# Scores of an attention kernel: one head in every second step, or two heads in every fourth

## The chip, the cores and the metric

The kernel runs on one core of a Trainium2 chip. The metric is the device time of one execution in microseconds (us). For the kernel before, three runs are shown, with a median of 1465.92 us.

## The reference

The tokens x are 64 sequences of 32 tokens with 512 features. Each sequence is mixed along its tokens by a 32x32 matrix, picked by a condition. Then come attention with 32 heads of 128 features (queries and keys normalised over all 4096 features), a residual, a linear layer with quantised weights and a low-rank update, and a gated low-rank expert layer with a residual:

```python
x = x + attn(einsum('bct,bcd->bdt', x, W[condition]))   # q, k = rms_norm(h @ Wq + bq), rms_norm(h @ Wk + bk)
                                                        # softmax(q k^T / sqrt(128)) v, then @ Wo + bo
x = x + ffn(cond2(x))                                   # quantised weight + lora; 8 experts, softmax gates
```

What matters here is q k^T: for each head and each sequence, a 32x32 block of scores from 32 queries and 32 keys with 128 features.

## The kernel before, in words

The queries and keys of the 32 heads are computed in 64 steps (`for s in range(N_QK)`, two steps a head, h = s // 2); the values follow in 32 further steps; then come softmax, values times probabilities, the output projection and the last layers. Two steps of a head cover the 2048 tokens, since a step treats a 1024-token half by a scheme of seven products: the 2x2 block product of (query and key weights) by (tokens) is made with seven products of half size instead of eight (p1 to p7, each six matmuls of 128x512 on TensorE: hi and lo parts of the operands, L672), and the results are put together from sums of products. A step delivers four blocks of 128x512: q_lo (block_11, L1687), q_hi (block_12, L1713), k_hi (block_22, L1700) and k_lo (ACT, L1224).

Each engine runs a list in a fixed order, written out by hand, and semaphores tie the lists together:

- TensorE, per step: p6(s), p5(s), p1(s+1), p7(s), in even steps `scores(s // 2 - 1)`, p2(s+1), p4(s), p3(s). `scores(h)` (L791) is 64 products of 128x32 by 128x32, each recorded as two instructions, in four column groups of the array, into bank 3 or 7. It uses the blocks of both steps of head h. In the steps of the values a product is twelve matmuls of 128x256 (L683).
- ACT: keep_a2(s) (L1115, behind p6), square and gain of q_hi(s-1), square and gain of q_lo(s) (L1136, L1142), a split of weights (L1052), keep_a3(s) (L1124, behind p7), keep_a1(s+1) (L1106), square of k_hi(s), k_lo(s).
- DVE: block_12(s-1), one threshold level of the quantised weights (L1653 and L1654, `level`), low_qk(6) in odd steps or low_qk(3) in even ones (L1548), block_22(s), in even steps keep_scores (L1672), low_qk(7) in odd steps, block_11(s+1), in steps with s % 6 == 1 a second level, low_qk(4) or low_qk(1). Steps 2 to 6 have small preparing operations in place of levels (`code_scales`, `code_steps`, `normalised`, `code_order`, `first_level`).
- POOL: in each step the additions of the squares (L1454, `add_square`), and sums of the next weights (`add_qk`).
- SP: loads of weights (`load_raw`) and the stores of scores to memory (`spill`).

p4(s) waits for a3_kept(s), p3(s) for c22_done(s) (block_22). block_22 of an even step waits for `scored`, since it writes over a block of keys that the scores read. Blocks of queries and keys live in `qk` (two of each kind), with a third place for q_lo in `sqst`. `keep_scores` copies a bank to `stage`, SP stores it, and `kept` frees the bank. `lora(0)` in step 3 writes banks 3 and 7 too.

```python
blk = {(name, par): qk[:, (2 * i + par) * 512:(2 * i + par + 1) * 512]
       for i, name in enumerate(("q_lo", "q_hi", "k_lo", "k_hi")) for par in range(2)}
blk["q_lo", 2] = sqst[:, 3, :]
...
def levels_qk(s):
    return 0 if s < 6 or s > 59 else 2 if s > 6 and s % 6 == 1 else 1
```

Of the kernel before, what the change touches and what calls it, by code (L numbers as in the profile page):

```python
# [9 lines left out]
ACT = mybir.ActivationFunctionType  # L10
AX = mybir.AxisListType.X

P = 128
# [71 lines left out]
def build(nc, x_nat, x_tr, cond_w, cond_idx, codebook, wqk, wv_in, wo_in, vecs, bo, w2, scale_log,  # L85
# [4 lines left out]
    with ExitStack() as ctx:  # L90
# [33 lines left out]
        wraw = sb("wraw", [P, 2048])  # L124
        accr = sb("accr", [P, 4096])

        with ExitStack() as mem_a:
# [11 lines left out]
        with ExitStack() as mem_b:  # L139
# [30 lines left out]

        blk = {(name, par): qk[:, (2 * i + par) * 512:(2 * i + par + 1) * 512]
               for i, name in enumerate(("q_lo", "q_hi", "k_lo", "k_hi")) for par in range(2)}
        blk["q_lo", 2] = sqst[:, 3, :]
        acc = accr[:, :].rearrange("p (a n) -> p a n", a=2)
# [228 lines left out]
        def _(sp):  # L403
# [49 lines left out]
            for s in range(1, N_QK):  # L453
                if s % 2 == 1 and (s + 3) // 2 < H:
                    load_raw((s + 3) // 2)
                if s == N_QK - 3:
                    load_v_raw(0, 0)
                if s == N_QK - 2:
                    load_v_raw(0, 1)
                if s % 2 == 0:  # L460
                    sp.wait_ge(kept, s // 2)
                    sp.dma_start(spill[s // 2 - 1], stage).then_inc(spilled, 16)

            sp.wait_ge(kept, H)
            sp.dma_start(spill[H - 1], stage).then_inc(spilled, 16)

# [27 lines left out]
            for s in range(N_QK, N_ST):  # L494
# [19 lines left out]
                if s == N_QK:  # L514
                    store_v(s, 11, c11_done)
                store_v(s, 22, c22_done)
                if u == 1:
# [78 lines left out]
        def _(pe):  # L596
# [176 lines left out]
            def scores(h):  # L773

                dst = bank[3 + 4 * (h % 2)]
                if h >= 2:
                    pe.wait_ge(kept, h - 1)
                if h == 1:
                    pe.wait_ge(lora_used, 2)
# [4 lines left out]
                for n in range(NCH):  # L784
                    s, part = 2 * h + n % 2, ("lo", "hi")[n // 2]
                    q, k = blk["q_" + part, s % (3 if part == "lo" else 2)], blk["k_" + part, s % 2]
                    for t in range(TC):
                        for j in range(NB):
                            cols = slice(t * P + j * C, t * P + (j + 1) * C)
                            at = (n * TC + t) * C  # L790
                            ins = pe.matmul(dst[j * C:(j + 1) * C, at:at + C], q[:, cols], k[:, cols],  # L791
                                            start=True, stop=True)
# [20 lines left out]
            for s in range(N_QK):  # L813
# [13 lines left out]
                p7(s)  # L827
                if s % 2 == 0:
                    scores(s // 2 - 1)
                p2(s + 1)  # L830
                if s == 3:
                    pe.wait_ge(kept, 1)
                    lora(0)
# [35 lines left out]
            p5(N_QK)  # L869
            p6(N_QK)  # L870
            scores(H - 1)
            for s in range(N_QK, N_ST):
# [157 lines left out]
        def _(act):  # L1030
# [23 lines left out]
            def split_v(j, q):  # L1054
# [15 lines left out]
                elif j == 6:  # L1070
                    act.wait_ge(scored, H - 1)
                elif j == 7:
                    act.wait_ge(p_done[3], N_QK)
                else:
                    act.wait_ge(scored, H)
# [64 lines left out]
            def gain(name, s, ready):  # L1140
                q = blk[name, s % (3 if name == "q_lo" else 2)]
                act.activation(q, q, ACT.Copy, scale=vec[:, s // 2, 3:4]).then_inc(ready, 1)  # L1142

            def last_q(s):

                act.wait_ge(c12_done, s + 1)
                square(sq_q_hi(s), 0, s % 2 + 2, blk["q_hi", s % 2], None)

# [39 lines left out]
            for s in range(N_QK):  # L1188
# [8 lines left out]
                act.wait_ge(c11_done, s + 1)  # L1197
                square(sq_q_lo(s), 0, s % 2, blk["q_lo", s % 3], None)
                gain("q_lo", s, gq_lo)
# [19 lines left out]
                act.wait_ge(c22_done, s + 1)  # L1219
                square(sq_k_hi(s), 1, s % 2 + 2, blk["k_hi", s % 2], None)  # L1220
                if s % 2 == 0 and s >= 2 and h + 1 < H:
                    split_qk(1, h + 1)
                act.wait_ge(p_done[4], s + 1)
                act.activation(blk["k_lo", s % 2], bank_a(s)[:, :], ACT.Identity, bias=vec[:, h, 1:2], scale=1.0)\  # L1224
                   .then_inc(c21_done, 1)
# [302 lines left out]
        def _(dve):  # L1528
# [145 lines left out]
            def block_11(s):  # L1674
                dve.wait_ge(p_done[2], s + 1)
                dve.wait_ge(a1_kept, s + 1)
                if s < N_QK:
                    dst = blk["q_lo", s % 3]
                    if s == 2:
                        dve.wait_ge(t_lo, t_at(2, 7))  # L1680
# [8 lines left out]
            def block_22(s):  # L1689
                dve.wait_ge(p_done[5], s + 1)  # L1690
                dve.wait_ge(a3_kept, s + 1)
                if s < N_QK:
                    dst = blk["k_hi", s % 2]
                    if s % 2 == 0:
                        dve.wait_ge(scored, s // 2)
                else:
# [5 lines left out]
            def block_12(s):  # L1702
                dve.wait_ge(p_done[3], s + 1)
                dve.wait_ge(a2_kept, s + 1)
                if s < N_QK:
                    dst = blk["q_hi", s % 2]
                else:
# [43 lines left out]
            for s in range(N_QK):  # L1751
# [32 lines left out]
                if s >= 2:  # L1784
                    block_22(s)
                if s % 2 == 0 and s >= 2:
                    keep_scores(s // 2 - 1)
                if s % 2 == 1 and h + 1 < H:
# [29 lines left out]
            low_v(7)  # L1818
            keep_scores(H - 1)
            low_v(4)  # L1820
# [67 lines left out]
            for s in range(N_QK, N_ST):  # L1888
                u = s - N_QK
                block_22(s)  # L1890
                if s + 1 < N_ST:
                    block_11(s + 1)
# [205 lines left out]
```

## Time and profile before

| what | value |
|---|---|
| median of the runs shown | 1465.92 us (1465.64 to 1467.06) |
| span of the profiled execution | 1464.0 us |
| instructions | 37072 |
| TensorE matmul busy | 1459.2 us, 15683 instructions |
| VectorE (DVE) busy | 1089.7 us (74%) |
| ScalarE (ACT) busy | 726.7 us (50%) |
| GpSimd (POOL) busy | 752.5 us (51%) |
| TensorE clock granted | 1.000 |

The profiled execution gives the span from its first to its last instruction; a device time of its own is not given beside it. The median of the runs lies 1.9 us above the span. TensorE counts as busy while a matmul drains, so its idle time says little, and the starts of its instructions say more. In a timeline row stand the start in us from the beginning of the span, the duration in us, engine, line, operation, what is written and read, shapes and the number of instructions merged, and in brackets the idle time of the engine before it and what ended it.

### The profile page before, as it was taken

How to read it: one execution, taken by the hardware profiler on the slowest of the kernel's cores; microseconds unless marked ns; L12 is line 12 of the kernel's file. 1: busy time of each engine (PE TensorE's matmuls, PEld its weight loads, DVE VectorE, ACT ScalarE, POOL GpSimd, SP SyncE). 2: the span in 40 equal slices, each digit the busy share in tenths (PEclk: the TensorE clock that was granted, in tenths of full speed). 3: DMA queues.
4: the chain of work that ended last, by engine and by line, in shares of the span. 5: the costliest groups of instructions: out<-in, count | busy, mean ns of one | idle time of the engine just before them, and what ended most of it. 6: DMA issues, size and time to landing. Idle time of an engine off the chain costs nothing.

```text
span 1464.0 us, 37072 instructions
## 1 busy us (share of the span) xinstructions
PE 1459.2 (100%) x15683; PEld 1262.6 (86%) x15683; DVE 1089.7 (74%) x1505; ACT 726.7 (50%) x1330; POOL 752.5 (51%) x532
## 2 busy tenths in 40 slices
PE   9999999999999999999999999999999999999999
PEld 8788888888888888888999999999888888888887
DVE  8787868788786877874498889988677676667663
ACT  7767677666767667675333333344443222222221
POOL 7667777787777877775444444454453112112100
PEclk9999999999999999999999999999999999999999
DMA  4211111110111101111433433447474244244230
GB/s 151 66 44 45 38 36 38 45 45 31 37 45 45 44 24 44 45 44 59 153 129 131 143 128 133 137 155 228 151 233 131 83 135 131 74 136 140 73 116 30
DMA packets 106998, 135.28 MB, mean 92 GB/s; under 512 B 6224, under 2 KB 89424, under 8 KB 106320
## 3 DMA queue, kind: packets, MB, share of 16 engines
q1 hardware_dynamic: 105968, 132.49, 27.4%
q8 instruction: 123, 2.02, 0.6%
q10 hardware_dynamic: 864, 0.42, 0.1%
q14 instruction: 43, 0.35, 0.1%
HBM read 86.75 MB, written 46.14 MB: 91 GB/s over the span
## 4 chain that ended last, share of the span: by engine, by line
PE 96%; DVE 2%; ACT 1%; issue 1%; DVEq 0%; POOL 0%; ACTq 0%; POOLq 0%
PE bank L672 39%; PE bank L906 24%; PE bank L683 22%; PE bank L865 4%; PE bank L791 3%; PE bank L934 1%; PE bank L952 1%; PE bank L621 0%; DVE qreg L1654 0%; DVE wa L1548 0%; PE bank L600 0%; DVE xs_lo L1611 0%; DVE qreg L1633 0%; PE bank L963 0%; PE bank L920 0%
## 5 line engine op out<-in xcount | busy, mean ns | idle before, releaser
L672 PE MATMUL bank<-xs_hi,wa 128*128 128x512 f32 x1792 | 563.4, 392 | 0.2
L1454 POOL TENSOR_TENSOR accr<-accr,sqst 128x512 f32<-128x512 f32 x248 | 352.8, 1433 | 148.1 <-ACT sqst L1136 108.4
L672 PEld LDWEIGHTS bank<-xs_hi,wa 128*128 128x128 f32 x1792 | 336.3, 188 | 74.3 <-DVE qk L1700 2.4
L672 PE MATMUL bank<-xs_lo,wa 128*128 128x512 f32 x896 | 348.6, 389 | 0.0
L683 PE MATMUL bank<-wv,xs_hi 128*128 128x256 f32 x1792 | 323.3, 283 | 0.1
L906 PE MATMUL bank<-ot,wo_main 128*128 128x512 f32 x1344 | 316.6, 392 | 0.0
L906 PEld LDWEIGHTS bank<-ot,wo_main 128*128 128x128 f32 x1344 | 249.5, 188 | 52.6
L683 PEld LDWEIGHTS bank<-wv,xs_hi 128*128 128x128 f32 x1792 | 279.6, 192 | 2.2 <-issue 1.9
L683 PE MATMUL bank<-wv,xs_lo 128*128 128x256 f32 x896 | 253.5, 283 | 0.0
L1548 DVE TENSOR_TENSOR wa<-wraw,wa 128x256 fp32r<-128x256 f32 (+1 forms) x160 | 157.5, 985 | 96.5 <-ACT wa L1052 94.7
L1261 ACT ACTIVATE ot<-bank,vec 128x256 fp32r<-128x256 f32 x256 | 100.3, 476 | 239.4 <-PE bank L906 146.4
L1881 DVE SCALAR_TENSOR_TENSOR ot<-bank,vec,ot 128x256 fp32r<-128x256 f32 x256 | 106.2, 478 | 135.9 <-ACT ot L1261 135.7
L672 PEld LDWEIGHTS bank<-xs_lo,wa 128*128 128x128 f32 x896 | 168.3, 188 | 33.2
L683 PEld LDWEIGHTS bank<-wv,xs_lo 128*128 128x128 f32 x896 | 172.0, 192 | 0.0
L1494 POOL TENSOR_TENSOR wraw<-wraw,rinv 128x1024 f32<-128x1024 f32 x16 | 30.6, 1915 | 269.6 <-DVE rinv L1863 269.6
L1136 ACT ACTIVATE sqst<-qk 128x512 f32<-128x512 f32 x165 | 103.5, 627 | 62.9 <-DVE qk L1700 39.3
L1875 DVE STREAM_TRANSPOSE weights_b<-wraw 32x256 f32<-32x256 f32 x256 | 111.3, 435 | 3.5
L1654 DVE TENSOR_TENSOR accr<-accr,qreg 128x1024 f32<-128x1024 f32 x63 | 106.4, 1689 | 2.2
L1654 DVE TENSOR_TENSOR qreg<-qreg 128x1024 f32<-128x1024 f32 x63 | 103.9, 1650 | 2.2
L1052 ACT ACTIVATE wa<-wraw 128x256 fp32r<-128x256 f32 (+1 forms) x160 | 79.0, 494 | 3.2 <-PE bank L672 3.2
L1115 ACT ACTIVATE snap<-bank,vec 128x512 f32<-128x512 f32 x64 | 44.2, 690 | 72.1 <-PE bank L672 72.1
L1142 ACT ACTIVATE qk<-qk,vec 128x512 f32<-128x512 f32 x107 | 76.1, 711 | 0.0
(222 smaller groups left out, 1729.3 us busy)
## 6 DMA issues: line engine op xcount, KB each, us to landing
values_b<-v_spill SPq DMA_DIRECT2D x62, 512.0 KB, 4.8
wraw<-in_wqk SPq DMA_DIRECT2D x32, 512.0 KB, 3.6
v_spill<-vo SPq DMA_DIRECT2D x64, 256.0 KB, 2.3
v_spill<-sqst SPq DMA_DIRECT2D x64, 256.0 KB, 2.3
score_spill<-sqst SPq DMA_DIRECT2D x32, 256.0 KB, 2.0
wraw<-in_wv SPq DMA_DIRECT2D x16, 512.0 KB, 5.1
wraw<-score_spill SPq DMA_DIRECT2D x16, 512.0 KB, 4.1
accr<-in_wo SPq DMA_DIRECT2D x16, 512.0 KB, 5.9
```

Of the source, the lines that this page charges most:

```text
L672: ins = pe.matmul(dst[:, :], wa[:, col:col + P], xpart[:, j - 1, kt, n * CH:(n + 1) * CH], start=(first and k == 0), stop=(k == 5), skip_g ...
L683: ins = pe.matmul(dst[:, tp * 256:(tp + 1) * 256], xpart[:, j - 1, kt, t * P:(t + 1) * P], wv[:, col:col + 256], start=(first and k == 0), ...
L906: ins = pe.matmul(bank[i][:, :], wo_slot(p)[:, wpart, col:col + P], ot[:, b % 2, opart, h, :], start=(p == 0 and k == 0), stop=(p == NP - ...
L1052: act.activation(wa[:, col:col + n], wraw[:, src:src + n], ACT.Copy).then_inc(w_hi[g], 1)
L1136: act.activation(dst, src, ACT.Square).then_inc(sq_ready, 1)
L1142: act.activation(q, q, ACT.Copy, scale=vec[:, s // 2, 3:4]).then_inc(ready, 1)
L1261: ins = act.activation(ot_part(ot[:, b % 2, 0, h, :], r), pv_part(b, r, h), ACT.Identity, bias=vec[:, 2 * (b % NP) + h, 2:3], scale=1.0)
L1454: pool.tensor_tensor(a, a, sq_slot(count), ALU.add).then_inc(acc_done, 1)
L1548: dve.tensor_tensor(wa[:, col + n:col + 2 * n], wraw[:, src:src + n], wa[:, col:col + n].bitcast(F32), ALU.subtract).then_inc(w_lo[g], 1)
L1654: link(dve.tensor_tensor(qf[half], qf[half], qm, ALU.add))
L1875: ins = dve.transpose(pt[rows, b % 2, :, :, j * C:(j + 1) * C], src)
L1881: ins = dve.scalar_tensor_tensor(out=ot_part(ot[:, b % 2, 1, h, :], r), in0=pv_part(b, r, h), scalar=vec[:, 2 * (b % NP) + h, 2:3], in1=ot ...
```

## The change

The scores are made for two heads in one visit of TensorE, in steps 4, 8 and so on to 60, and for the last two heads behind p6(64). A second tensor of query and key blocks, `qk_more`, holds four blocks of each kind (five of q_lo). Its place, 16 KB a partition, comes from the scratch for dynamic DMAs, which is cut to 64 bytes. `keep_scores` and the stores of the scores follow in steps 4n and 4n + 1, and for the last head in the first step of the values. The waits on `scored` and `kept` are set to match.

```diff
--- before.py
+++ after.py
@@ -123,6 +123,7 @@
 
         wraw = sb("wraw", [P, 2048])
         accr = sb("accr", [P, 4096])
+        qk_more = sb("qk_more", [P, 4096])
 
         with ExitStack() as mem_a:
             snap = mem_a.enter_context(nc.sbuf_tensor("snap", [P, 4, 512], F32))
@@ -168,9 +169,12 @@
         tt_of = [tt[0], tt[1], {**tt[0], 4: qk[:, 2560:3072]}, tt[1]]
 
 
-        blk = {(name, par): qk[:, (2 * i + par) * 512:(2 * i + par + 1) * 512]
-               for i, name in enumerate(("q_lo", "q_hi", "k_lo", "k_hi")) for par in range(2)}
-        blk["q_lo", 2] = sqst[:, 3, :]
+        SLOTS = {"q_lo": 5, "q_hi": 4, "k_lo": 4, "k_hi": 4}
+        blk = {}
+        for i, name in enumerate(SLOTS):
+            for par in range(4):
+                blk[name, par] = (qk_more, qk)[par // 2][:, (2 * i + par % 2) * 512:(2 * i + par % 2 + 1) * 512]
+        blk["q_lo", 3], blk["q_lo", 4] = sqst[:, 3, :], blk["q_lo", 3]
         acc = accr[:, :].rearrange("p (a n) -> p a n", a=2)
         stage = sqst[:, 4, :]
         a1, a3, a2 = snap[:, 0, :], snap[:, 2, :], (snap[:, 1, :], snap[:, 3, :])
@@ -457,12 +461,13 @@
                     load_v_raw(0, 0)
                 if s == N_QK - 2:
                     load_v_raw(0, 1)
-                if s % 2 == 0:
-                    sp.wait_ge(kept, s // 2)
-                    sp.dma_start(spill[s // 2 - 1], stage).then_inc(spilled, 16)
-
-            sp.wait_ge(kept, H)
-            sp.dma_start(spill[H - 1], stage).then_inc(spilled, 16)
+                if s >= 4 and s % 4 < 2:
+                    h = s // 4 * 2 - 2 + s % 4
+                    sp.wait_ge(kept, h + 1)
+                    sp.dma_start(spill[h], stage).then_inc(spilled, 16)
+
+            sp.wait_ge(kept, H - 1)
+            sp.dma_start(spill[H - 2], stage).then_inc(spilled, 16)
 
             def store_v(s, c, done):
                 u = s - N_QK
@@ -513,6 +518,9 @@
                     load_wo(1)
                 if s == N_QK:
                     store_v(s, 11, c11_done)
+                if s == N_QK:
+                    sp.wait_ge(kept, H)
+                    sp.dma_start(spill[H - 1], stage).then_inc(spilled, 16)
                 store_v(s, 22, c22_done)
                 if u == 1:
                     sp.wait_ge(stat_done, 1)
@@ -775,7 +783,7 @@
                 dst = bank[3 + 4 * (h % 2)]
                 if h >= 2:
                     pe.wait_ge(kept, h - 1)
-                if h == 1:
+                if h == 0:
                     pe.wait_ge(lora_used, 2)
                 pe.wait_ge(gq_lo, 2 * h + 2)
                 pe.wait_ge(c21_done, 2 * h + 2)
@@ -783,7 +791,7 @@
                 pe.wait_ge(c22_done, 2 * h + 2)
                 for n in range(NCH):
                     s, part = 2 * h + n % 2, ("lo", "hi")[n // 2]
-                    q, k = blk["q_" + part, s % (3 if part == "lo" else 2)], blk["k_" + part, s % 2]
+                    q, k = blk["q_" + part, s % SLOTS["q_" + part]], blk["k_" + part, s % 4]
                     for t in range(TC):
                         for j in range(NB):
                             cols = slice(t * P + j * C, t * P + (j + 1) * C)
@@ -825,11 +833,11 @@
                 p5(s)
                 p1(s + 1)
                 p7(s)
-                if s % 2 == 0:
+                if s % 4 == 0:
+                    scores(s // 2 - 2)
                     scores(s // 2 - 1)
                 p2(s + 1)
                 if s == 3:
-                    pe.wait_ge(kept, 1)
                     lora(0)
                 p4(s)
                 p3(s)
@@ -868,6 +876,7 @@
 
             p5(N_QK)
             p6(N_QK)
+            scores(H - 2)
             scores(H - 1)
             for s in range(N_QK, N_ST):
                 if s > N_QK:
@@ -1068,7 +1077,7 @@
                 elif j == 5:
                     act.wait_ge(p_done[5], N_QK)
                 elif j == 6:
-                    act.wait_ge(scored, H - 1)
+                    act.wait_ge(scored, H - 2)
                 elif j == 7:
                     act.wait_ge(p_done[3], N_QK)
                 else:
@@ -1138,13 +1147,13 @@
                     act.activation(dst, src, ACT.Square, bias=bias, scale=1.0).then_inc(sq_ready, 1)
 
             def gain(name, s, ready):
-                q = blk[name, s % (3 if name == "q_lo" else 2)]
+                q = blk[name, s % SLOTS[name]]
                 act.activation(q, q, ACT.Copy, scale=vec[:, s // 2, 3:4]).then_inc(ready, 1)
 
             def last_q(s):
 
                 act.wait_ge(c12_done, s + 1)
-                square(sq_q_hi(s), 0, s % 2 + 2, blk["q_hi", s % 2], None)
+                square(sq_q_hi(s), 0, s % 2 + 2, blk["q_hi", s % 4], None)
 
             x_block(0, 0)
             x_block(1, 0)
@@ -1195,7 +1204,7 @@
                 if s == 1:
                     keep_a3(s)
                 act.wait_ge(c11_done, s + 1)
-                square(sq_q_lo(s), 0, s % 2, blk["q_lo", s % 3], None)
+                square(sq_q_lo(s), 0, s % 2, blk["q_lo", s % 5], None)
                 gain("q_lo", s, gq_lo)
                 h = s // 2
                 if s % 2 == 1 and h + 1 < H:
@@ -1217,11 +1226,11 @@
                     difference(2, 4)
                     difference(3, 4)
                 act.wait_ge(c22_done, s + 1)
-                square(sq_k_hi(s), 1, s % 2 + 2, blk["k_hi", s % 2], None)
+                square(sq_k_hi(s), 1, s % 2 + 2, blk["k_hi", s % 4], None)
                 if s % 2 == 0 and s >= 2 and h + 1 < H:
                     split_qk(1, h + 1)
                 act.wait_ge(p_done[4], s + 1)
-                act.activation(blk["k_lo", s % 2], bank_a(s)[:, :], ACT.Identity, bias=vec[:, h, 1:2], scale=1.0)\
+                act.activation(blk["k_lo", s % 4], bank_a(s)[:, :], ACT.Identity, bias=vec[:, h, 1:2], scale=1.0)\
                    .then_inc(c21_done, 1)
                 square(sq_k_lo(s), 1, s % 2, bank_a(s)[:, :], vec[:, h, 1:2])
                 if s == 0:
@@ -1675,8 +1684,8 @@
                 dve.wait_ge(p_done[2], s + 1)
                 dve.wait_ge(a1_kept, s + 1)
                 if s < N_QK:
-                    dst = blk["q_lo", s % 3]
-                    if s == 2:
+                    dst = blk["q_lo", s % 5]
+                    if s == 3:
                         dve.wait_ge(t_lo, t_at(2, 7))
                 else:
                     dst = v_out[11]
@@ -1690,9 +1699,9 @@
                 dve.wait_ge(p_done[5], s + 1)
                 dve.wait_ge(a3_kept, s + 1)
                 if s < N_QK:
-                    dst = blk["k_hi", s % 2]
-                    if s % 2 == 0:
-                        dve.wait_ge(scored, s // 2)
+                    dst = blk["k_hi", s % 4]
+                    if s % 4 == 0 and s >= 4:
+                        dve.wait_ge(scored, s // 2 - 1)
                 else:
                     dst = v_out[22]
                     if s > N_QK:
@@ -1703,7 +1712,7 @@
                 dve.wait_ge(p_done[3], s + 1)
                 dve.wait_ge(a2_kept, s + 1)
                 if s < N_QK:
-                    dst = blk["q_hi", s % 2]
+                    dst = blk["q_hi", s % 4]
                 else:
                     dst = v_out[12]
                     if s == N_QK:
@@ -1783,8 +1792,8 @@
                     low_v(2)
                 if s >= 2:
                     block_22(s)
-                if s % 2 == 0 and s >= 2:
-                    keep_scores(s // 2 - 1)
+                if s >= 4 and s % 4 < 2:
+                    keep_scores(s // 4 * 2 - 2 + s % 4)
                 if s % 2 == 1 and h + 1 < H:
                     low_qk(7, h + 1)
                 if s + 1 < N_QK:
@@ -1816,7 +1825,7 @@
             low_v(6)
             block_12(N_QK - 1)
             low_v(7)
-            keep_scores(H - 1)
+            keep_scores(H - 2)
             low_v(4)
             block_11(N_QK)
             low_v(3)
@@ -1888,6 +1897,8 @@
             for s in range(N_QK, N_ST):
                 u = s - N_QK
                 block_22(s)
+                if s == N_QK:
+                    keep_scores(H - 1)
                 if s + 1 < N_ST:
                     block_11(s + 1)
                 if u == 1:
@@ -2084,7 +2095,7 @@
         "bmat": a["L0_ffn_B"].transpose(0, 2, 1).reshape(E_ * R_, D),
         "br": np.broadcast_to(a["L0_ffn_br"], (P, E_)),
     }
-    nc = bacc.Bacc("TRN2", target_bir_lowering=False, num_devices=1)
+    nc = bacc.Bacc("TRN2", target_bir_lowering=False, num_devices=1, dynamic_dma_scratch_size=64)
     arrays, args = {}, []
     for name, v in laid.items():
         v = np.ascontiguousarray(v)
```

## Rows read from the trace of the kernel before

**Rows 1.** The page, part 4: the chain that ended last, by engine.
```profile
PE 96%; DVE 2%; ACT 1%; issue 1%; DVEq 0%; POOL 0%; ACTq 0%; POOLq 0%
```

**Rows 2.** Waits of TensorE, whole span: waited for, us in total, times, longest.
```profile
PE bank L791 <- ACT qk L1142: 0.3, 1, 0.3
```

**Rows 3.** Timeline of ACT: keep_a2 of steps 24 to 27. Columns: start us, us, engine.
```profile
273.01 0.69 ACT L1115 ACTIVATE snap<-bank,vec 128x512 f32<-128x512 f32 x1 [1.15 <-PE bank L672]
...
283.97 0.69 ACT L1115 ACTIVATE snap<-bank,vec 128x512 f32<-128x512 f32 x1 [1.45 <-PE bank L672]
...
293.49 0.69 ACT L1115 ACTIVATE snap<-bank,vec 128x512 f32<-128x512 f32 x1 [1.15 <-PE bank L672]
...
304.60 0.69 ACT L1115 ACTIVATE snap<-bank,vec 128x512 f32<-128x512 f32 x1 [0.77 <-PE bank L672]
```

**Rows 4.** Timeline of TensorE around the scores visit of step 22.
```profile
256.19 0.39 PE L672 MATMUL bank<-xs_hi,wa 128*128 128x512 f32 x1
256.51 0.46 PE L791 MATMUL bank<-qk,sqst 128*32 128x32 f32 x32
256.79 1.02 PE L791 MATMUL bank<-qk 128*32 128x32 f32 x96
257.74 0.51 PE L672 MATMUL bank<-xs_hi,wa 128*128 128x512 f32 x1
258.08 0.39 PE L672 MATMUL bank<-xs_lo,wa 128*128 128x512 f32 x1
```

**Rows 5.** Timeline of TensorE: two pv blocks, then the 0.3 us window 1058.7:1059.0 alone.
```profile
1057.90 2.10 PE L865 MATMUL bank<-weights_b,values_b 64*64 64x64 f32 x128
...
1058.48 0.73 PE L865 MATMUL bank<-weights_b,values_b 64*64 64x64 f32 x35
```

**Rows 6.** Timeline of DVE in step 24.
```profile
276.63 0.46 DVE L1548 TENSOR_TENSOR wa<-wraw,wa 128x256 fp32r<-128x256 f32 x1 [0.42 <-ACT wa L1052]
278.42 0.69 DVE L1700 TENSOR_TENSOR qk<-bank,snap 128x512 f32<-128x512 f32 x1 [1.32 <-PE bank L791]
```

**Rows 7.** Timeline of ACT in step 24: keep_a3.
```profile
277.09 0.69 ACT L1124 ACTIVATE snap<-bank,vec 128x512 f32<-128x512 f32 x1 [0.56 <-PE bank L672]
```

**Rows 8.** Timeline of DVE in steps 25 and 26.
```profile
288.84 0.69 DVE L1700 TENSOR_TENSOR qk<-bank,snap 128x512 f32<-128x512 f32 x1 [0.19 <-ACT snap L1124]
...
290.38 1.73 DVE L1653 TENSOR_SCALAR qreg<-qreg,thr,step 128x1024 f32<-128x1024 f32 x1
...
299.48 1.41 DVE L1548 TENSOR_TENSOR wa<-wraw,wa 128x256 fp32r<-128x256 f32 x1
300.81 0.68 DVE L1700 TENSOR_TENSOR qk<-bank,snap 128x512 f32<-128x512 f32 x1
```

**Rows 9.** Timeline of DVE: block_22 of steps 2, 3 and 6.
```profile
52.11 0.68 DVE L1700 TENSOR_TENSOR qk<-bank,snap 128x512 f32<-128x512 f32 x1
...
63.31 0.69 DVE L1700 TENSOR_TENSOR qk<-bank,snap 128x512 f32<-128x512 f32 x1
...
95.17 0.68 DVE L1700 TENSOR_TENSOR qk<-bank,snap 128x512 f32<-128x512 f32 x1
```

**Rows 10.** Timeline of ACT: keep_a2 of steps 2, 3, 4, 6 and 7.
```profile
45.41 0.69 ACT L1115 ACTIVATE snap<-bank,vec 128x512 f32<-128x512 f32 x1 [0.54 <-PE bank L672]
...
56.37 0.69 ACT L1115 ACTIVATE snap<-bank,vec 128x512 f32<-128x512 f32 x1 [1.23 <-PE bank L672]
...
67.19 0.69 ACT L1115 ACTIVATE snap<-bank,vec 128x512 f32<-128x512 f32 x1 [1.06 <-PE bank L672]
...
87.66 0.69 ACT L1115 ACTIVATE snap<-bank,vec 128x512 f32<-128x512 f32 x1 [1.15 <-PE bank L672]
...
98.97 0.69 ACT L1115 ACTIVATE snap<-bank,vec 128x512 f32<-128x512 f32 x1 [0.77 <-PE bank L672]
```

**Rows 11.** Timeline of POOL in steps 25 and 26.
```profile
290.27 1.29 POOL L1454 TENSOR_TENSOR accr<-accr,sqst 128x512 f32<-128x512 f32 x1 [2.18 <-ACT sqst L1136]
...
296.70 3.90 POOL L1454 TENSOR_TENSOR accr<-accr,sqst 128x512 f32<-128x512 f32 x2
```

## The prediction

> **What bounds the kernel now.** I read first the chain that ended last. TensorE has 96% of the 1464.0 us span on it [rows 1], so a change is worth what it takes from TensorE's own queue, or what it makes that queue wait; DVE, ACT and POOL count only where they are late for it. The waits of TensorE in the stretch of queries and keys look empty: the largest is 0.3 us before one scores visit [rows 2]. This is deceptive, since TensorE is busy while a matmul drains, so the next view is the length of the steps. keep_a2(s) on ACT starts when p6(s) is done, once a step: steps 24, 25 and 26 take 10.96, 9.52 and 11.11 us [rows 3]. An odd step has seven products of six matmuls, 42 in 9.52 us, 0.227 us each. An even step has a scores visit more. Step 26 is 0.15 us longer than step 24, and that excess is the clue for what follows.
>
> **What one visit costs.** In step 22 the last wide matmul before the visit starts at 256.19, the scores at 256.51, the next wide ones at 257.74 and 258.08 [rows 4]. From 256.19 to 258.08 are 1.89 us, where two wide matmuls would take 0.45: the visit costs 1.43 us. Its 128 instructions run from 256.51 to the last start at 257.61 (256.79 + 1.02 less the 0.20 that one lasts), 1.10 us, 8.7 ns each. So 0.33 us per visit is entering and leaving the narrow form: 0.09 before it, 0.12 after its last start and 0.12 in the first wide matmul behind it. The second head of a double visit should cost 1.10 us and no 0.33. What passes between two heads (five waits, another bank) no row of the scores shows. The nearest is pv(b) followed by pv(b+1): 128 instructions in 2.10 us less the 0.22 that one lasts, 14.8 ns each, and the 0.3 us window around the change from b to b+1 has 35 of them in 0.73 us, again 15 ns each [rows 5]. The change of pair costs nothing there. I take 0 for the handover, with 0.33 as the other end (each head pays for a whole visit).
>
> **What is moved.** Sixteen heads (those scored in steps 2, 6, 10 to 62) leave their step, 1.43 us each if nothing else holds it; sixteen second heads arrive in steps 4, 8 to 60 and behind p6(64), 1.10 us each. Without stalls that is 16 x 0.33 = 5.3 us gained. The stalls decide.
>
> **Where a removed visit is worth its price.** p3(s) waits for block_22(s), which follows keep_a3(s), which follows p7(s). The visit sat between p7 and p3 and so was cover. In step 24 DVE has finished low_qk(3) at 277.09 (276.63 + 0.46) and then waits 1.32 us for the scores, though ACT's keep_a3 is done at 277.78 [rows 6, 7]. Without the visit block_22 runs from 277.8 to 278.5. In a step without a visit p3 starts 6.60 us after keep_a2 (9.52 less p3 and p6, 1.36 each, less 0.20 from p6's end to keep_a2), 279.61: 1.1 us to spare. Ten source steps are like this one (10, 18, 22, 30, 34, 42, 46, 54, 58, 62): 14.3 us gained.
>
> **Where it is worth nothing.** Step 25 has two threshold levels on DVE (s % 6 == 1), and from block_22(25) at 288.84 on DVE is never idle until block_22(26) ends at 300.81 + 0.68 = 301.49 [rows 8]. Nothing in this chain waits for scores. p3(26) wants to start at 293.49 + 6.60 = 300.09 once the visit is gone, but starts 0.09 behind block_22 as before, 301.58: 1.49 us of stall stand where the visit stood. keep_a2(27) comes at 304.60 as now. Steps 14, 26, 38, 50 gain 0. Step 6 is the same: p3 could start at 87.66 + 6.60 = 94.26, block_22(6) ends at 95.85 behind DVE's threshold ordering [rows 9, 10]; 11.31 us become about 11.2, 0.1 gained. In step 2, p3 could start at 45.41 + 6.60 = 52.01, block_22(2) ends at 52.79, so p3 starts at 52.88 instead of 53.45 (2.92 before the next keep_a2). But DVE is as late in step 3, where small operations keep block_22(3) until 64.00 [rows 9], so p3(3) moves from 64.27 to 64.09: 0.2 gained for both steps.
>
> **What the destination steps give back.** Steps 20, 32, 44, 56 are today's 26 with a visit, 0.15 us late; step 8 has that and the 0.3 us wait for the gain of q_hi [rows 2]. A second head of 1.10 us is more cover than that: 5 x 0.15 + 0.3 = 1.0 us of old stalls go.
>
> **The moved copy.** keep_scores of the second head goes from even steps to steps 5, 9, 13 and so on, behind block_22. It holds DVE for 0.60 us (its 0.68 less overlap with the next). In most of those steps DVE idles later. In steps 5, 13, 25, 37, 49 it stands at the head of the very chain that sets p3 of the step behind. There I look at what the chain waits for: the level's tensor_scalar of 290.38 lasts 1.73 us; POOL's addition beside it ends at 291.56, and 0.55 us later DVE is through. Likewise low_qk(3) of 299.48 ends at 300.89, 0.29 behind POOL's addition, which ends at 300.60 [rows 8, 11]. DVE waits for POOL, so starting the tensor_scalar at 290.98 instead of 290.38 still ends it near 292.1. I take 0 for the copy; the other end is 0.60 in each of five steps, 3.0 us.
> The Trainium skill ("SBUF — State Buffer", Who interferes with whom) says that VectorE and GpSimd share a pair of ports under an exclusive lock, that whichever issues first holds it for the whole instruction, and that a DVE instruction with at most one SBUF input outside the two-port modes is not blocked. By that rule the copy out of PSUM slips under a wait that is there anyway, and the sum stays as it is; were the long durations plain slowness, the sum would be 3.0 us higher. The trace agrees with the lock in the two places above.
>
> **Covered or free.** The wait of block_22 for scored comes earlier and only every fourth step; behind it on DVE are the copy, block_11 and low_qk(1), all due over 1 us later. On SP the spills move by steps, and behind them stands load_raw, whose weights are wanted only by the next head. ACT's gains and squares keep their order; POOL's eight operations of an even step run 1.4 us closer to the next, and its additions are waited for only by squares three further. lora(0) loses a wait on a copy that is long done. At the end, p6(64) is followed by two heads; low_v(7), the last waiting for the scores, stays the same distance from them, and keep_scores of the last head adds 0.60 us on DVE in a step of wide V products. The smaller scratch changes no queue that carries data here: all loads go out from SP and ACT. If any cover is gone its cost is the copy's 0.6 us, once.
>
> **Sum.** 16 x 1.10 = +17.6; ten sources -14.3; steps 2 and 3 -0.2; step 6 -0.1; steps 14, 26, 38, 50 0; old stalls -1.0. Net +2.0 us on the span of 1464.0. The median of the runs shown, 1465.92, lies 1.9 above that span, and I put the 2.0 on it: **1467.9 us**. A measurement of this kernel can tell about 0.2%, 2.9 us, from no change.
>
> **Rivals.**
> Faster: the chain DVE and POOL form in the two-level steps gets shorter once the phases shift, since the waits for POOL in it (1.2 us in the tensor_scalar alone) are a matter of who comes first. If all stalls go, the gain is 5.3 + 2.0 (today's: 0.4 in step 6, 0.4 in step 8, 8 x 0.15) = 7.3 us: 1458.6. If half of them go, 1462. Against it: those operations of POOL hang on ACT's squares, and these on the same products as before. Chance 0.17.
> Slower by the copy: in steps 5, 13, 25, 37, 49 the 0.60 us reaches p3 of the next step, five times: +5.0, 1470.9. It decides against a tie from 0.2 us a step on. For it, DVE's chain there has no idle time; against it, the waits for POOL. Chance 0.20.
> Slower by the handover: the five waits between heads cost up to the 0.33 of a visit, 16 times: up to 1473.2, near 1469.5 with a third of it. Chance 0.08.
> The change doesn't do what it says, or the scratch touches a queue: chance 0.03, within 0.2% mostly.
> My forecast, between 1466.5 and 1469.5, keeps 0.52; of it 0.07 lies over the 0.2%, and the faster rival has 0.03 inside it.
> Together: faster 0.15, same 0.50, slower 0.35. The range takes in the copy's bound above and half of the faster rival below: 1462.5 to 1471.5.
>
> **What would show it.** Right: 16 visits of 256 instructions, each some 2.2 us from first to last start; steps without a visit of 9.52 us, but steps 14, 26, 38, 50 of about 11.1 us and step 6 of 11.2; steps 8, 20, 32 of 12.1; block_22's idle time behind scores gone from steps 4n+2. Wrong: step 26 near 9.5 (the faster rival), near 11.7 (the copy), or a gap between the 128th and the 129th instruction of a visit (the handover).

## The result, and the profile after

The change made the kernel slower: 1511.6 us median (1508.14 to 1516.38) against 1466.18 us, a ratio of 1.0312 with a 95% interval of [1.0292, 1.0332]. I had predicted 1467.9 us and a range up to 1471.5. Work is unchanged, 15683 matmul instructions before and after; the profiled execution spans 1508.4 us, 44.4 us more.

From the page of the changed kernel (parts 1, 3 and 4), and its waits of TensorE (waited for, us in total, times, longest):

```profile
span 1508.4 us, 37071 instructions
...
PE 1469.5 (97%) x15683; PEld 1270.4 (84%) x15683; DVE 1082.0 (72%) x1505; ACT 726.5 (48%) x1330; POOL 757.3 (50%) x532
...
q8 instruction: 123, 2.02, 0.5%
...
PE 91%; DVE 4%; issue 3%; ACT 2%; DVEq 0%; POOL 0%; ACTq 0%; POOLq 0%
```

```profile
PE bank L799 <- issue: 29.6, 16, 2.2
```

TensorE's share of the chain fell from 96% [rows 1] to 91%, and "issue" rose from 1% to 3%: time in which the engine waits for nothing that the profile shows. TensorE's own waits on "issue", 29.6 us, are all in the 16 scores visits (L799 is their line now), up to 2.2 us in one. The first of them, step 4, in the timeline of TensorE (compare [rows 4]):

```profile
71.08 1.30 PE L799 MATMUL bank<-qk_more 128*32 128x32 f32 x128
72.33 0.43 PE L799 MATMUL bank<-qk 128*32 128x32 f32 x29
...
74.97 0.75 PE L799 MATMUL bank<-qk 128*32 128x32 f32 x62 [1.87 <-issue]
75.65 0.50 PE L680 MATMUL bank<-xs_hi,wa 128*128 128x512 f32 x1
```

The visit begins as predicted, and the second head starts at 72.33. Then TensorE stops at 72.91 in the middle of the second head (128 + 66 = 194 matmuls in, 62 to go) and resumes at 74.97. What arrives meanwhile, in the DMA view of 71.6 to 75.0 us (a packet row gives packets, MB and share):

```profile
q1 hardware_dynamic: 62, 0.13, 9.8%
q8 instruction: 1, 0.02, 1.8%
```

The 62 packets belong to the store of the scores and come in the last 0.4 us of the window. Before them there is one packet of 0.02 MB of instructions. Over the whole span this queue brings 2.02 MB in 123 packets, 16.4 KB each. TensorE has 15683 weight loads and as many matmuls, 31366 instructions, so it is one packet for some 255 of them, 64 bytes each (216 semaphore instructions stand among them in its queue). This stood on the page of before too, and I had not read it.

Where the 44.4 us are, from the starts of matmuls in the timelines (a gap is the time from one start to the next):

| part | us |
|---|---|
| the long gap in each of 16 visits, 1.72 to 2.40, mean 2.05 | 32.7 |
| the gap at the 129th matmul of a visit, 0.155 to 0.31 | 3.1 |
| four stretches of 3.4 us at half clock, 1.7 each | 6.8 |
| what I had forecast for the rest | 2.0 |

That makes 44.6. The stretches at half clock come behind long gaps, as in this window view of 251.1 to 254.4 us, behind the visit of step 20 (the number behind the engines is the granted clock, 0.50, the 1.2 GHz level; the engine had just stood still for 2.3 us inside the visit). The row has 9 matmuls in 3.3 us, where 0.227 us each would give 14:

```profile
251.10:254.40 3.30, 3.30 (x9) 2.52 (x9) 0.77 (x2) 0.63 (x1) 1.21 (x1) 0.50 0.21 79
```

The rest went as forecast. keep_a2 of steps 24 to 27 of the changed kernel (compare [rows 3]):

```profile
286.73 0.69 ACT L1124 ACTIVATE snap<-bank,vec 128x512 f32<-128x512 f32 x1 [1.15 <-PE bank L680]
...
302.76 0.69 ACT L1124 ACTIVATE snap<-bank,vec 128x512 f32<-128x512 f32 x1 [1.46 <-PE bank L680]
...
312.28 0.69 ACT L1124 ACTIVATE snap<-bank,vec 128x512 f32<-128x512 f32 x1 [1.15 <-PE bank L680]
...
323.38 0.69 ACT L1124 ACTIVATE snap<-bank,vec 128x512 f32<-128x512 f32 x1 [0.77 <-PE bank L680]
```

Step 26, now without a visit, still takes 11.10 us, as I had said; step 25 takes 9.52. Step 24 takes 16.03 instead of 12.1: one gap and one stretch at half clock.

### The profile page after: what moved, and what is told of

Read it like the earlier page. It is cut to its first block, busy times and chain, and to the rows that moved or that the text cites. A ratio compares the mean times of both kernels' runs of the same rounds, so it can differ in the third digit from the quotient of the medians.

```text
span 1508.4 us, 37071 instructions
## 1 busy us (share of the span) xinstructions
PE 1469.5 (97%) x15683; PEld 1270.4 (84%) x15683; DVE 1082.0 (72%) x1505; ACT 726.5 (48%) x1330; POOL 757.3 (50%) x532
## 3 DMA queue, kind: packets, MB, share of 16 engines
q8 instruction: 123, 2.02, 0.5%
## 4 chain that ended last, share of the span: by engine, by line
PE 91%; DVE 4%; issue 3%; ACT 2%; DVEq 0%; POOL 0%; ACTq 0%; POOLq 0%
PE bank L680 36%; PE bank L915 24%; PE bank L691 21%; PE bank L873 4%; PE bank L799 3%; DVE qreg L1663 1%; PE bank L943 1%; PE bank L961 1%; DVE qreg L1662 0%; ACT snap L1133 0%; ACT qk_more L1151 0%; DVE wa L1557 0%; PE bank L629 0%; DVE qk L1709 0%; PE bank L608 0%
## 5 line engine op out<-in xcount | busy, mean ns | idle before, releaser
L1463 POOL TENSOR_TENSOR accr<-accr,sqst 128x512 f32<-128x512 f32 x248 | 358.2, 1456 | 182.1 <-ACT sqst L1145 106.5
L691 PE MATMUL bank<-wv,xs_lo 128*128 128x256 f32 x896 | 254.4, 284 | 0.0
L1557 DVE TENSOR_TENSOR wa<-wraw,wa 128x256 fp32r<-128x256 f32 (+1 forms) x160 | 147.0, 920 | 97.0 <-ACT wa L1061 95.6
L1662 DVE TENSOR_SCALAR qreg<-qreg,thr,step 128x1024 f32<-128x1024 f32 x63 | 79.6, 1264 | 0.0
L1145 ACT ACTIVATE sqst<-qk 128x512 f32<-128x512 f32 x89 | 55.8, 627 | 34.4 <-DVE qk L1709 19.5
```

Of the source, the lines that this page charges most:

```text
L691: ins = pe.matmul(dst[:, tp * 256:(tp + 1) * 256], xpart[:, j - 1, kt, t * P:(t + 1) * P], wv[:, col:col + 256], start=(first and k == 0), ...
L1463: pool.tensor_tensor(a, a, sq_slot(count), ALU.add).then_inc(acc_done, 1)
L1557: dve.tensor_tensor(wa[:, col + n:col + 2 * n], wraw[:, src:src + n], wa[:, col:col + n].bitcast(F32), ALU.subtract).then_inc(w_lo[g], 1)
L1662: link(dve.tensor_scalar(qm, qv[half], thr[:, t + 1:t + 2], step[:, t:t + 1], ALU.is_gt, ALU.mult))
```

## The experiments

**The theory.** (A) TensorE's instructions come in blocks of 256 (128 weight loads and 128 matmuls). The next block is fetched only when the one before it is begun, and this takes about 3.4 us (measured below: 3.0 to 3.8 in the changed kernel). Wide matmuls of 0.227 us need 29 us for a block. Narrow ones of 8.7 ns need 1.1 us, so a run of narrow matmuls that crosses two block boundaries stands still at the second. Rivals: the new storage or scratch (B); the change of head or bank inside a visit (C); no such boundary at all (D, E).

### Storage alone, and two heads apart

The storage of the change with single visits:

```diff
-                if s % 4 == 0:
-                    scores(s // 2 - 2)
+                if s % 2 == 0:
                     scores(s // 2 - 1)
...
-            scores(H - 2)
             scores(H - 1)
```

(and keep_scores, the stores and the waits on `kept` as in the kernel before)

> The storage of the change (second tensor of blocks, scratch of 64 bytes), but one head per visit in every even step as in the kernel before. Theory A (the time is lost because TensorE's instructions of a long narrow visit are not fetched in time): visits have 128 instructions again, no gap of 2 us in any, 1466 us, within 2 us of the kernel before. Rival B (new addresses of the blocks, or the small scratch, slow reading or a queue): 1500 us or more.

Measured: 1466.93 us against 1467.02, ratio 0.9999 [0.999, 1.0009], and no wait of TensorE on "issue". Storage, addresses and scratch cost nothing. Rival B is out.

The changed kernel with the second head behind p4:

```diff
                 if s % 4 == 0:
                     scores(s // 2 - 2)
-                    scores(s // 2 - 1)
                 p2(s + 1)
...
                 p4(s)
+                if s % 4 == 0:
+                    scores(s // 2 - 1)
```

> The changed kernel with the second head of a pair moved behind p4 of the same step: 32 visits of 128 instructions again, all in steps 4n, with 12 wide matmuls between the two. Theory A: no 2 us gaps; the cost is that of my forecast plus entering and leaving 16 times more, +2.0 + 16 x 0.33 = +7.3 on the span of before, 1471 us of span, 1473 measured. Rival C (two heads in one step, whatever lies between them): 1500 us or more.

Measured: 1476.67 us, ratio 1.0065 [1.005, 1.008], span 1475.3. Its waits of TensorE on "issue":

```profile
PE bank L799 <- issue: 2.3, 1, 2.3
```

One wait is left of 16. It is in the visit behind p6(64), which I had forgotten: there the two heads still stand together. Its gap of 2.5 us and one stretch at half clock (1.7) explain the 4 us above the expectation; +7.3 + 2.5 + 1.7 makes 1475.5. So two heads in one step are harmless, and two heads in one run are not.

### Fewer products, and products twice

The changed kernel with half of each head's products left out (half of the scores is not computed):

```diff
-                    for t in range(TC):
+                    for t in range(0, TC, 2):
```

> The changed kernel with half of each head's products left out (every second tile of sequences), so that a visit for two heads has 128 instructions; half of the scores are not computed. Theory A (length of the run of narrow instructions): the gaps of 2 us go, and with them the stretches at half clock; 1508.4 - 32.7 - 6.8 - 16 x 1.1 = 1451 us of span, a few us more if a boundary of the instruction blocks falls on some visits. Rival C (the change of head or bank inside a visit costs the 2 us): the gaps stay, span near 1485 to 1491.

Measured: span 1453.3 us (1455.23 median, 0.992 [0.99, 0.9939]). No wait on "issue" of 2 us is left. The change of head is still inside each visit, and costs the 0.155 us that it cost before. Rival C is out.

The kernel before, with the products of each head issued twice:

```diff
-                for n in range(NCH):
+                for m in range(2 * NCH):
+                    n = m % NCH
```

> The kernel before, single visits in every even step, with each head's products issued twice to the same place: visits of 256 matmul instructions, with neither the new storage nor a second head. Theory A: each of 32 visits gets 1.1 us more of work and a gap of about 2 us: 1464 + 35 + 65 = 1564 us of span, more if stretches at half clock follow. Without a fetch limit: 1464 + 35 = 1499.

Measured, in one run: 1594.1 us, span 1592.3. Its waits:

```profile
PE bank L792 <- issue: 72.1, 32, 3.0
```

All 32 visits stand still, with single heads and the old storage. The gaps sum to 78 us (mean 2.45 against 2.05 in the change, more than expected), 35 us are the doubled work, and eleven stretches at half clock bring some 19: 132 in all, for the measured 128. The 1564 us that theory A gave had 65 us of gaps and no such stretch.

### Is it a boundary or a length?

If blocks have 256 instructions, the place of the gap must follow from counting. In the changed kernel the gaps of the first nine visits lie behind matmul 194, 152, 238, 196, 154, 240, 198, 156, 242. From one visit's start to the next there are 168 wide matmuls and 256 narrow ones, so 848 instructions, and 4 more if each step has one further queue instruction. From the first gap to the second are 852 + 2 x (152 - 194) = 768 = 3 x 256 instructions, from there to the third 852 + 2 x (238 - 152) = 1024 = 4 x 256. All 15 gaps in the steps share one remainder. Counted over the whole trace, with the semaphore instructions of TensorE's queue where they stand, the one behind p6(64) has it too, and so do the 32 gaps with doubled products among themselves.

The packets fit as well. By the count, the boundary before the one at which TensorE stands still in step 4 is passed at 71.66 us. The view of 72.6 to 73.7 us, in 40 slices of 0.0275 us, has the packet in its third slice, at 72.66:

```profile
GB/s 0 0 596 0 0 0 0 0 0 0 0 0 0 0 0 0 0 0 0 0 0 0 0 0 0 0 0 0 0 0 0 0 0 0 0 0 0 0 0 0
```

TensorE goes on at 74.97, and the next packet starts at 76.11, 1.1 us behind that. In all 16 visits the packet starts 0.7 to 1.2 us behind the first boundary and TensorE goes on 2.3 to 2.8 us behind the packet, together 3.0 to 3.8 us, 3.3 in the mean. Among wide matmuls it is different: in steps 5 to 63 of the kernel before, the packet starts 1.0 to 4.4 us ahead of the boundary, so the queue is read ahead of the matmuls there. With the count the boundaries can be computed, and moved.

The kernel before with six more small matmuls in the prologue, each recorded as two, so 12 matmul instructions:

```diff
-            for i in range(8):
+            for i in range(14):
```

> The kernel before, with six narrow matmuls (12 instructions, 0.1 us) more in the prologue and nothing else, which moves the boundaries of TensorE's 16 KB instruction blocks against the scores visits by 12 instructions. Theory A: in every third visit (heads 0, 3, 6 ...) a boundary lay some 11 instructions inside the visit and the next one as far behind it, 3.5 us later, just enough; now both lie at the visit's ends, 1.5 to 2.6 us apart, and up to eleven visits show a gap of 0.5 to 1.7 us: +5 to +15 us. Rival D (no such boundary matters): +0.1 us.

Measured: 1467.18 us, 1.0001 [0.9991, 1.0011]. Nothing moved. I had placed the boundary 11 matmuls inside the visits from a guess about when a packet is asked for. The count from the gaps gives 24 to 33 for every third visit, and a shift by 12 is then not enough. The next run used the count:

```diff
-            for i in range(8):
+            for i in range(22):
```

> The kernel before with fourteen narrow matmuls (28 matmul instructions, 0.3 us) more in the prologue. Why the shift by 12 did nothing: in the changed kernel all 15 gaps of 2 us between products lie at one place modulo 256 of TensorE's queue instructions (weight loads, matmuls, and one more instruction a step). By that count a block boundary lies 24 to 33 matmuls inside every third visit of the kernel before, and the next boundary as many wide matmuls behind the visit, far more than the 10 that are needed to fill 3.4 us; a shift by 12 still leaves 12 to 21. A shift by 28 leaves -4 to 5. Theory A: about ten visits (heads 3, 6, 9 and so on) show a gap of 1 to 2 us at their end or within five matmuls behind it: +8 to +20 us. Rival D (no boundary matters for single visits): +0.3 us.

Measured: 1491.74 us, ratio 1.018 [1.016, 1.02], span 1489.2. Fourteen small matmuls in the prologue cost 26 us, more than the 8 to 20 that were expected: most gaps are of 2.0 to 2.6 us instead of 1 to 2, and stretches at half clock come on top. Its waits of TensorE and the scores visit of step 14:

```profile
PE bank L791 <- issue: 9.2, 5, 2.4
PE bank L672 <- issue: 7.5, 4, 2.4
```

```profile
175.57 1.25 PE L791 MATMUL bank<-qk 128*32 128x32 f32 x124
178.87 0.26 PE L791 MATMUL bank<-qk 128*32 128x32 f32 x4 [2.04 <-issue]
179.05 0.50 PE L672 MATMUL bank<-xs_hi,wa 128*128 128x512 f32 x1
```

The gap stands behind the 124th of 128 matmuls. In the following visits of this kind (heads 9, 12, 15) it stands behind the 125th, 126th and 127th, then (heads 18 to 27) directly behind the visit and one, two and three wide matmuls later. Head 0 has a short one of 0.6 us, heads 3 and 30 none. Nine gaps sum to 19.1 us, and four stretches at half clock to 6.8: 25.9 for the measured 25.2. A single visit of 128 is therefore not safe by its length, only by its place, and rival D is out.

The changed kernel with three quarters of the products (a quarter of the scores is not computed), visits of 192:

```diff
-                    for t in range(TC):
+                    for t in range(TC - 1):
```

> The changed kernel with the last quarter of each head's products left out (a quarter of the scores isn't computed): visits of 192 matmul instructions, blocks of 128. By the count of instructions the visits numbered 3, 4, 5, 9, 10, 11 (from 0) hold two block boundaries: theory A expects the gap of about 2 us in these, at their matmul 132, 154, 176, 136, 158, 180. Visits 0, 6, 12 have the second boundary 2 to 10 wide matmuls behind their end: a gap of 0.3 to 1.8 us there. The others show none. Rival E (a visit above some length between 128 and 256 always stalls, or never does): all visits alike.

Measured, in one run: 1478.71 us, span 1476.9. Visit 4 of it (counted from 0), in parts:

```profile
236.53 0.40 PE L799 MATMUL bank<-qk_more 128*32 128x32 f32 x24
...
240.50 0.76 PE L799 MATMUL bank<-qk 128*32 128x32 f32 x38 [2.28 <-issue]
```

192 - 38 = 154, the matmul that was named. Visits 5, 10, 11 have their gaps at 176, 158, 180, as named; visits 0 and 6 have 1.7 and 1.1 us ahead of the third and seventh wide matmul behind their end, and visit 15, which was not named, has 0.5 us at its matmul 126. Visits 3, 9 and 12 were expected to have a gap and have none. In 3 and 9 the first boundary lies 5 and 9 matmuls inside the visit, and its packet had started 2.0 us before that boundary, ahead of the visit. These two visits used up both boundaries in 1.24 us and did not stand still. In the shifted kernel the packet of the eight visits with long gaps started 0.8 to 1.7 us behind the boundary, though that lay just as near the visit's start; these visits had a wait for ACT there (0.35 us between the last wide matmul's start and the first narrow one's, elsewhere 0.32). That this wait is the difference is argued, not shown: head 3 of the shifted kernel has such a wait too (0.64 us from start to start), with the boundary four wide matmuls ahead of the visit, and there the packet comes 3.4 us ahead of the boundary and no gap follows. Rival E is out, since equal visits differ.

### The handover, and the stall terms

The waits of the second head issued ahead of the first:

```diff
+                if h % 2 == 0:
+                    if h >= 2:
+                        pe.wait_ge(kept, h)
...
+                    pe.wait_ge(gq_hi, 2 * h + 4)
+                    pe.wait_ge(c22_done, 2 * h + 4)
```

> The changed kernel with the five waits of the second head issued ahead of the first head. It measures the handover by itself: at the 128th instruction of each visit there is now a gap of 0.155 to 0.31 us, 3.1 us in 16 visits. If the waits make it, it falls to the 0.03 us that stands at the start of a visit, and the rest of the kernel stays (gaps of 2 us and 1508 us less 3). If the new bank or head makes it, it stays at 0.155.

Measured: the gap at the 129th matmul is gone (0.155 us or more before, 0.015 us or less now in 15 of 16 visits; in the other a block's gap of 0.7 us falls on it), so the waits make it. But the kernel is slower still: 1526.81 us, span 1528.0. The long gaps have grown to a mean near 2.5 us and TensorE is at half clock for 41 us in all, in eleven stretches, instead of 13.7 us in four. A part of the growth is arithmetic: in the changed kernel the handover, 0.20 us in the mean, lay between the two boundaries in all 16 visits, so it passed while the block was on its way, and without it the gap is longer by as much. The rest is open: from boundary to resumption it takes 3.3 to 4.0 us here in most visits, where it took 3.0 to 3.8.

The kernel before with the level of steps 8, 14, 20 to 56 put at the end of DVE's list, to test the chain of my stall terms:

```diff
+                late = s > 7 and s % 6 == 2 and levels_qk(s) == 1
...
-                if levels_qk(s):
+                if levels_qk(s) and not late:
                     level(0, taken)
                     taken += 1
...
+                if late:
+                    level(0, taken)
+                    taken += 1
```

> The kernel before, single visits; in steps 8, 14, 20 to 56 (s % 6 == 2) the threshold level stands at the end of the step's list on DVE instead of ahead of low_qk(3) and block_22. It tests the chain on which my stall terms rest: block_22 is then early, so the 0.15 us by which these eight steps are longer (and most of the 0.43 us of step 8) should go: steps 14, 20, 26 of 10.95 us, span 1464.0 - 1.3 = 1462.7 us, measured 0.1% faster at most. If the chain is another (ACT or POOL), these steps stay at 11.1 us. Risk: block_12 of the next step comes 2 us later, and odd steps behind could grow beyond 9.52 us.

Measured: 1473.17 us, ratio 1.0048 [1.0034, 1.0062], span 1471.9, where 1462.7 was expected. block_22 of step 26 is early now, and the step takes 11.01 us instead of 11.11; but the step behind takes the risk that was named. keep_a2 of steps 26, 27 and 28:

```profile
296.51 0.69 ACT L1115 ACTIVATE snap<-bank,vec 128x512 f32<-128x512 f32 x1 [1.15 <-PE bank L672]
...
307.52 0.69 ACT L1115 ACTIVATE snap<-bank,vec 128x512 f32<-128x512 f32 x1 [1.45 <-PE bank L672]
...
317.95 0.69 ACT L1115 ACTIVATE snap<-bank,vec 128x512 f32<-128x512 f32 x1 [0.98 <-PE bank L672]
```

Step 27 has 10.43 us instead of 9.52, nine times 0.9 us. So the order of DVE's list sets the length of steps 26 and 27, and the order of the kernel before is the better one. No run here that computes everything beats the kernel before.

## Why the prediction was wrong

Point by point:

- **What a visit costs** (1.43 us, of which 1.10 are the head's): right for single visits.
- **The price of the second head** is the step that failed: the term 16 x 1.10 us, with 0 for the handover. The 1.10 us came from a visit of one head [rows 4], the 0 (0.33 as the other end) from pv(b) and pv(b+1) [rows 5]. Measured are 0.15 to 0.31 at the change of head (16 times, 3.1 us) and, inside the second head at the next block boundary, 2.05 us (16 times, 32.7 us); a visit takes 4.1 to 5.1 us from first to last start instead of 2.2. With the waits out of the way the 3.1 us did not come back, since the gaps grew by more. The analogue was wrong in just the quantity that matters: a pair of pv blocks has 128 matmuls in 1.9 us, one block of instructions in all, while two heads have 256 in 2.2 us. The bound above was taken from the cost of a visit; a limit that no visit of before had reached was not in it, and the sign I named, a gap between the 128th and the 129th instruction, stands in the wrong place for the large one.
- **The stretches at half clock** (6.8 us) were not in the prediction. They go with the gaps: without a long gap no run shows one while TensorE still has work.
- **Removed visits worth 1.43 us**: right. The ten steps named (10, 18, 22 and so on) take 9.52 us.
- **Removed visits worth nothing**: right. Steps 14, 26, 38 and 50 take 11.11 us (11.1 forecast), step 6 takes 11.36 (11.2 forecast).
- **Steps 2 and 3**: small, but the wrong way. 0.2 us were to be gained; they take 10.82 and 11.19 us against 10.95 and 10.82 [rows 10], 0.24 more.
- **Old stalls of the destination steps**: gone as forecast, for p3 waits for nothing in them.
- **The moved copy**: 0 was right. DVE in steps 25 and 26 of the changed kernel:

```profile
308.24 0.68 DVE L1681 COPY sqst<-bank 128x512 f32<-128x512 f32 x1
...
309.77 1.19 DVE L1662 TENSOR_SCALAR qreg<-qreg,thr,step 128x1024 f32<-128x1024 f32 x1
...
319.60 0.68 DVE L1709 TENSOR_TENSOR qk<-bank,snap 128x512 f32<-128x512 f32 x1
```

  The copy is there, the tensor_scalar starts 0.6 us later and lasts 1.19 us instead of 1.73 [rows 8]. Counted from keep_a2(25) it ends at 8.20 us, where it had ended at 8.14. POOL's addition beside it (309.07, 1.34 us) ends at 310.41, and 0.55 us later DVE is through, as before. The Trainium skill ("SBUF — State Buffer", Who interferes with whom) has VectorE and GpSimd share a pair of ports under an exclusive lock; the trace agrees with it: DVE's start moved by 0.60 us and its end by 0.06.
- **The scratch and the storage**: free, as forecast.

The net of all forecast terms was +2.0 us. With the gaps, the handover and the stretches at half clock taken off, the measured budget leaves 44.4 - 32.7 - 3.1 - 6.8 = 1.8 for them.

## What to carry to other kernels

Count the instructions of a run of short ones against the packets of the instruction queue: here a block of 128 weight loads and 128 matmuls took 3.0 to 3.8 us to come, and all 16 double visits, which passed two block boundaries faster than that, stood still at the second. Two visits of 192 matmuls, whose first packet had come early, did not. Gathering small matmuls into one visit saves the cost of entering (0.33 us here) and cost 2 us, and in 4 of 16 cases a stretch at half clock; 12 wide matmuls between the parts were enough to prevent it in 15 pairs of heads here. Such a kernel's time also depends on where its blocks fall, so that 28 matmul instructions in TensorE's prologue moved it by 1.8%, and a comparison of two kernels should look for "issue" waits before it looks for reasons.

## What was not expected of the hardware

- Instructions of TensorE came in packets of 16 KB, 123 for 31366 instructions, and the gaps shared one place modulo 256 instructions.
- Fourteen matmuls of 128x16 more in the prologue made the kernel 1.8% slower ([1.016, 1.02]); six more did nothing.
- After the gaps of the visits (1.7 to 2.4 us) the granted clock was 0.50, the 1.2 GHz level, for 3.4 us in 4 of 16 cases in the changed kernel, all behind gaps of 2.1 us or more, and in 11 of 32 (gaps of 2.2 us or more) with doubled products.
- Five waits between narrow matmuls cost 0.155 us when none of them had to wait for anything.
